# A 13x13 depthwise convolution by Toeplitz matmuls: weights of the last rows widened to 128 columns, patch halves requested together, shifted copies dropped

## The reference, cut to what matters

```python
# layer 0: 1x1 qkv convolution, 2x2 max pool, 3x3 depthwise, channel attention, projection (not touched)
x = x + _L0_conv_ref(_gn(x), ...)
# layer 1: what the changed stage computes, x is (1, 384, 192, 192) fp32
out = _bn(_dwconv(x, w_large, 6), ...) + _bn(_dwconv(x, w_small, 1), ...) + _bn(x, ...)   # w_large (384,1,13,13), w_small (384,1,3,3)
x = x + out(_gn(x))
```

## Time and profile before

| | |
|---|---|
| median of 3 runs | 2976.05 us (2973.62 to 2976.38) |
| the profiled execution's own time | 2976.38 us |
| its span | 2974.7 us |
| PE busy | 2670.8 us (90%) |
| DVE busy | 2522.6 us (85%) |
| ACT busy | 1481.1 us (50%) |
| bytes moved by DMA | 546.95 MB |

### The profile page before, as it was taken

One profiled execution on the slowest core, in us unless ns is written; L12 is line 12 of the kernel. 1 busy time (PEld: TensorE's weight loads), 2 busy tenths in 40 slices (PEclk: granted clock), 3 DMA queues, 4 the chain that ended last, 5 costly groups with the idle time before them and its releaser, 6 DMA issues. The chain is left out here.

```text
span 2974.7 us, 50705 instructions
## 1 busy us (share of the span) xinstructions
PE 2670.8 (90%) x17273; PEld 1812.0 (61%) x17273; DVE 2522.6 (85%) x3512; ACT 1481.1 (50%) x1921; POOL 73.9 (2%) x143
## 2 busy tenths in 40 slices
PE   0049999999999999999995999983999999999998
PEld 0036666666666666666663566652777777777776
DVE  7969999999999999999997898984877777777774
ACT  0033445555554554553232667673655555555553
POOL 0010000000000000000000000000000000000000
PEclk9999999999999999999997999995999999999999
DMA  8964112222322322321004999988999999999985
GB/s 333 416 204 144 49 56 93 85 87 84 103 77 93 103 77 87 100 81 48 17 1 152 333 349 346 343 291 177 251 263 261 261 262 261 261 262 260 262 249 169
DMA packets 349112, 546.95 MB, mean 184 GB/s; under 512 B 143392, under 2 KB 254752, under 8 KB 345888
## 3 DMA queue, kind: packets, MB, share of 16 engines
q1 hardware_dynamic: 317504, 436.49, 47.5%
q10 hardware_dynamic: 31456, 108.48, 11.8%
HBM read 364.47 MB, written 180.44 MB: 183 GB/s over the span
## 5 line engine op out<-in xcount | busy, mean ns | idle before, releaser
L781 PE MATMUL qk_qb<-qk_xhi,whi 128*128 128x384 f16 x2592 | 846.4, 327 | 21.0 <-DVE qk_xlo L677 14.3
L781 PE MATMUL qk_qb<-qk_xlo,whi 128*128 128x384 f16 x2592 | 846.2, 326 | 0.0
L781 PE MATMUL qk_qb<-qk_xhi,wlo 128*128 128x384 f16 x2592 | 846.2, 326 | 0.0
L698 DVE SCALAR_TENSOR_TENSOR qk_dw<-qk_pool,qk_wd,qk_dw 128x768 f32<-128x768 f32 (+2 forms) x864 | 836.9, 1009 | 0.1
L685 DVE TENSOR_REDUCE qk_pool<-qk_qb 128x192 f32<-128x768 f32 x432 | 411.9, 954 | 68.7 <-PE qk_qb L781 51.9
L1491 ACT ACTIVATE cv_res<-cv_cb,cv_cst 128x288 f32<-128x288 f32 x384 | 189.8, 502 | 381.5 <-PE cv_cb L1634 331.3
L1628 PE MATMUL cv_cb<-cv_hi,cv_toep 128*128 128x288 f16 x1536 | 346.6, 286 | 35.5 <-DVE cv_lo_last L1559 32.8
L781 PEld LDWEIGHTS qk_qb<-qk_xhi,whi 128*128 128x128 f16 x2592 | 254.0, 98 | 184.2 <-DVE qk_xlo L677 17.5
L781 PEld LDWEIGHTS qk_qb<-qk_xhi,wlo 128*128 128x128 f16 x2592 | 253.9, 98 | 168.4 <-issue 1.2
L1634 PE MATMUL cv_cb<-cv_hi_next,cv_toep 128*128 128x288 f16 x1536 | 356.3, 293 | 0.0
L781 PEld LDWEIGHTS qk_qb<-qk_xlo,whi 128*128 128x128 f16 x2592 | 254.0, 98 | 162.8 <-issue 1.0
(11 more groups left out here) (163 smaller groups left out, 3466.3 us busy)
## 6 DMA issues: line engine op xcount, KB each, us to landing
cv_toep<-toeplitz_scratch SPq DMA_DIRECT2D x384, 256.0 KB, 4.7
patch_scratch<-pr_turned SPq DMA_DIRECT2D x75, 832.0 KB, 9.6
st_x<-in_x SPq DMA_DIRECT2D x24, 2304.0 KB, 17.1
qk_xf<-in_x SPq DMA_DIRECT2D x72, 768.0 KB, 4.3
pr_xb<-in_x SPq DMA_DIRECT2D x24, 2304.0 KB, 10.1
out<-cv_rows ACTq DMA_DIRECT2D x72, 768.0 KB, 5.7
cv_raw<-patch_scratch SPq DMA_DIRECT2D x25, 1300.0 KB, 9.8
cv_raw<-patch_scratch ACTq DMA_DIRECT2D x23, 1300.0 KB, 9.5
```

Of the source, the lines that this page charges most:

```text
L698: V.scalar_tensor_tensor(acc, pool[:, o, r + y:r + y + n, x:x + PW], wd[:, o, k:k + 1], acc, ALU.mult, ALU.add).then_inc(taps_done, 1)
L781: ins = nc.tensor.matmul(qbank[s % NQB][:, h, 0:2 * W], w[:, b, o * P:(o + 1) * P], x[:, par, j // 2, b, at_row:at_row + 2 * W], start=n = ...
```

## The change

Three edits, all in `stage_depthwise`:

1. `late` gets a second half per channel, filled once with zeros by POOL. The weight view `few` then has 128 columns (64 real, 64 zero), and the three matmuls of row shift 2 write all 128 partitions of the bank. SP waits once for the zeros.
2. `hi_next`, `lo_next` and the copies `next_rows` go. The six matmuls of row shift 1 read `hi` and `lo` at row offset 1 of the pitch-26 rows.
3. SP requests its half of `raw` at c == 9 (behind the load of channel 8's weights) and ACT requests its half at c == 0 (right behind the first eviction, ahead of `last_high` of part 3).

```diff
-        hi_next = sb("hi_next", [P, GRP, TJ, OI], F16)
-        lo_next = sb("lo_next", [P, GRP, TJ, OI], F16)
-        late = sb("late", [P, GRP, ERUN], F16)
+        late = sb("late", [P, GRP, 2, ERUN], F16)
...
-                sp.dma_start(late[:, part_of(q), :],
+                sp.dma_start(late[:, part_of(q), 0, :],
...
-                    if c == GRP // 2 and (inner or g + 2 < NG):
+                    if c == NTOEP + 1 and (inner or g + 2 < NG):
                         address(sp, (g + 2) * (TI * GRP * TJ))
                         sp.wait_ge(edge_done, g * NPC + NPC)
                         start.load_half(sp, g + 2, par, 0)
                     if inner or g < NG:
                         load_taps(g, c)
+                        if at(g, 0) and c == 0:
+                            sp.wait_ge(late_zero, 1)
...
+        @block.gpsimd
+        def _(gp):
+            nc.gpsimd.memset(late[:, :, 1, :], 0.0).then_inc(late_zero, 1)
...
-                    if c == 0:
-                        last_high(g, NPC - 1)
-                    if c == GRP // 2 - 3 and (inner or g + 2 < NG):
+                    if c == 0 and (inner or g + 2 < NG):
                         address(act, (g + 2) * (TI * GRP * TJ))
                         act.wait_ge(edge_done, g * NPC + NPC)
                         start.load_half(act, g + 2, par, 1)
+                    if c == 0:
+                        last_high(g, NPC - 1)
...
-            def next_rows(g, q):
-                V.tensor_copy(hi_next[:, part_of(q)], hi[:, part_of(q), :, 1:1 + OI]).then_inc(hi_next_done, 1)
+            def last_low(g, q):
                 dve.wait_ge(lo_done, g * NPC + q + 1)
-                V.tensor_copy(lo_next[:, part_of(q)], lo[:, part_of(q), :, 1:1 + OI]).then_inc(lo_next_done, 1)
...
-                few = late[:, c, :].rearrange("p (m v) -> p v m", v=2)
+                few = late[:, c].rearrange("p r (m v) -> p v (r m)", v=2)
-                    nc.tensor.matmul(upper, few[:, part], x[:, c, :, 0:EI], start=False, stop=False, skip_group_check=True)
+                    nc.tensor.matmul(whole[:, :, 0:EI], few[:, part], x[:, c, :, 0:EI], start=False, stop=False, skip_group_check=True)
                 for u in range(NU):
-                    for k, (part, x) in enumerate(((0, hi_next), (0, lo_next), (1, hi_next))):
-                        ins = nc.tensor.matmul(whole, taps[:, 1, u * 2 + part], x[:, c, u:u + OJ, :],
+                    for k, (part, x) in enumerate(((0, hi), (0, lo), (1, hi))):
+                        ins = nc.tensor.matmul(whole, taps[:, 1, u * 2 + part], x[:, c, u:u + OJ, 1:1 + OI],
...
-                            for ready in (hi_next_done, lo_next_done, hi_last_done, lo_last_done):
+                            for ready in (hi_last_done, lo_last_done):
```

More of the change, by code:

```diff
@@ L1368, in stage_depthwise @@
         bbank = [ctx.enter_context(nc.psum_tensor(f"cv_bb{i}", [P, 512], F32)) for i in range(NBB)]
-        cst_in = sem("cst_in")
+        cst_in, late_zero = sem("cst_in"), sem("late_zero")
         toep_in = [sem(f"toep_in{i}") for i in range(NTOEP)]
@@ L1373, in stage_depthwise @@
         norm_done, edge_done, hi_done, lo_done = sem("norm_done"), sem("edge_done"), sem("hi_done"), sem("lo_done")
-        hi_next_done, lo_next_done, hi_last_done, lo_last_done = (sem("hi_next_done"), sem("lo_next_done"),
-                                                                  sem("hi_last_done"), sem("lo_last_done"))
+        hi_last_done, lo_last_done = sem("hi_last_done"), sem("lo_last_done")
         conv_done, res_done, back_done, rows_done = (sem("conv_done"), sem("res_done"), sem("back_done"),
@@ L1548, in low @@
                                 ALU.subtract).then_inc(lo_done, 1)
-            def next_rows(g, q):
-                V.tensor_copy(hi_next[:, part_of(q)], hi[:, part_of(q), :, 1:1 + OI]).then_inc(hi_next_done, 1)
+            def last_low(g, q):
                 dve.wait_ge(lo_done, g * NPC + q + 1)
-                V.tensor_copy(lo_next[:, part_of(q)], lo[:, part_of(q), :, 1:1 + OI]).then_inc(lo_next_done, 1)
-            def last_low(g, q):
                 for u in range(NU):
@@ L1575, in split @@
                 low(g, q)
-                next_rows(g, q)
                 last_low(g, q)
@@ L1622, in channel @@
                 taps = toep[:, c % NTOEP, :].rearrange("p (s m v) -> p s v m", s=NS, m=P)
-                few = late[:, c, :].rearrange("p (m v) -> p v m", v=2)
+                few = late[:, c].rearrange("p r (m v) -> p v (r m)", v=2)
                 whole = bank[:, 0:NPIX].rearrange("p (j i) -> p j i", j=OJ)
-                upper = bank[0:HP, 0:NPIX].rearrange("p (j i) -> p j i", j=OJ)[:, :, 0:EI]
                 for u in range(NU):
```

## The result

The changed kernel takes 2940.3 us (median of 4 runs, 2939.52 to 2940.88) against 2974.8; the ratio is 0.9885 (95% interval 0.9868 to 0.9902). That is faster, as forecast, but by 34 us where 88 were forecast, and outside the range of 2875 to 2925. The profiled execution has a span of 2938.3 us, 36.4 less than before.

What follows compares the result with a forecast made beforehand. PE alone was taken to bound the depthwise stage. Span 2974.7 - 94 (widened weights) + 5 (halves together) + 0 (start) = 2885.7 us, a median time of 2887; range 2875 to 2925.

Steps and rivals of the forecast that it cites:

- What bounds the kernel: Depthwise stage from about 2089 us on: PE alone sets the pace; DVE and ACT have room, DMA engines 8% left.
- Widened weights, 94 us: Row shift 2 matmuls: removing both width changes saves 0.25 us per channel over 376 channels, 94 us (bounds 92 and 98).
- No shifted copies, "I take nothing for it": Row shift 1 matmuls reading at an odd fp16 element: no cost taken; dropping DVE's copies worth nothing in the steady state.
- half-rate rival: Row shift 1: PE reads odd-offset rows at half rate, 276 us more, time 3158; chance 0.12.
- Patch halves together, 0.2 us per group: Channel 9's weights land late behind both halves: 0.2 us per group taken, 5 us in all (bounds 0 to 22).
- Start of the stage, 0: First depthwise channels: 3.4 us gained without copies is spent waiting for channel 9's weights; 0 taken, 3.4 either way.
- The range: Whole kernel: 2875 to 2925 us; high end takes in poor DMA meshing and the word per row with its stalls.
- the word per row: Row shift 1: each odd-offset row costs one more word, 0.01 us per matmul, 23 us, time 2910; chance 0.12.
- the late weights: Channel 9's Toeplitz weights behind both patch halves: PE waits at most 1 us per group, 22 us over 22 groups.
- the 5 in the sum: Depthwise stage: 5 us added to the forecast time for PE's waits caused by requesting the patch halves together.
- DMA-bound rival: Depthwise groups: busy DMA time cannot be compressed, a group takes 34.3 us, time 2906, up to 2920; chance 0.12.

Runs made afterwards that it cites:

- b_nocopy: Kernel before with only the shifted copies dropped, row shift 1 read at an odd element: 3000.76 us, ratio 1.0088.
- b_small_patch: Kernel before with widened weights only, and patch loads from group 2 on cut to their first row tile of 25: 2881.03 us, ratio 0.9685.
- b_widen: Kernel before with only the widened 128-column weights for row shift 2; copies kept, halves requested apart: 2891.29 us, ratio 0.9719; 2889.29 us in five more rounds.
- a_stagger: Changed kernel with the third edit undone, so patch halves are requested apart as before: 2912.62 us, ratio 0.9792.
- a_stag_even: Changed kernel with halves requested apart and row shift 1 reading at even row offset 0 instead of 1: 2886.49 us, ratio 0.9706.
- b_together: Kernel before with only the third edit, both patch halves requested after channel 0: 2977.67 us, ratio 1.0007.

## Why the prediction was wrong

- **What bounds the kernel**: right. PE alone; DVE's copies were worth nothing (b_nocopy).
- **Widened weights, 94 us**: right. 0.49 to 0.37 is seen directly. By the mean distances between the starts of matmuls from 2300 to 2800 us a channel is 0.243 us shorter and not 0.25, which makes 91 us. The 93 us of b_small_patch are these 91 and 2.5 us by which its channel 9 starts earlier (2086.7 us instead of 2089.2); b_widen has 83 to 85, by its waits. The drain on a change of tiling mode that the Trainium skill states (TensorEngine Tiling (Array Packing), Key Properties) agrees: with one mode throughout, both gaps went.
- **No shifted copies, "I take nothing for it"**: the first step that failed. The bound given beside it, 0.01 us per matmul and 23 us, was the right one (0.80 instead of 0.74 for six; 26 us in b_nocopy and between a_stagger and a_stag_even, 3 of them not placed). The argument for zero took DVE's reads at the same offset as evidence for PE. They were another engine's. The remark under the half-rate rival, that nothing else in the trace explains why packed shifted copies were kept, was the better evidence and should have decided against zero.
- **Patch halves together, 0.2 us per group**: the second step that failed, and the larger. The method was right: half issued, landing of the weights behind it, need of PE. In it the landing was taken as 18.1 us after channel 0 and is 19.5. Channel 0 ends at 2497.63 + 1.91 = 2499.5 (the chain's matmuls of the group before end at 2497.63). SP's half is issued 1.8 us later and not 1.0, because SP is held until 2500.1 by its issue of the late weights (2498.51, 1.56 us long), which was left out of what is queued ahead; and the weights land 17.7 us after the half's issue, not 17.1. (The medians of 21 groups are much the same: 1.9, 17.7 and together 19.6.) Need is at 1.91 + 7 x 2.34 = 18.3, so 1.2 us late per group (20 waits of 1.3 were measured) where 0.4 came out of the sum and 0.2 was taken. PE's next six matmuls then take 0.92 instead of 0.74, 0.18 more, so that the price per group is 1.4 to 1.5.
- The Trainium skill (SBUF — State Buffer, "Can I just issue two DMAs to hit both halves?") says that two such DMAs serialize and gain 6%. That they serialize agrees with the trace: SP's half lands after 17.3 us instead of 9.8. The 6% can't be read from it, since the rate hangs on the window and on what else moves: 241 GB/s from 2502 to 2510.5 with both halves in flight, 204 from 2503 to 2510, and 187 from 2511.5 to 2517 with SP's alone.
- **Start of the stage, 0**: near, but partly by luck. The prediction took 8 channels as done before 2089.18 us; the trace has 9, and it is channel 9 that starts there. So the need for channel 9's weights was put 2 us too late (2087.6; channel 8 ended at 2085.5), and their landing 1.4 us too late (2091; it was 2089.62), and the errors nearly cancel. PE got there 3.7 us earlier, waited 4.2 us and started channel 9 at 2089.67, 0.5 us later than before. The wait had a second price: in the 5 us from 2089 the mean granted clock is 0.66, a part of it at the 1.2 GHz level, and twice six matmuls take 1.44 us. Together with the start that is 2 us lost.

```profile
2089.67 0.93 PE cv_cb L1624 x6
2090.59 0.62 PE cv_cb L1627 x3
2091.21 1.44 PE cv_cb L1630 x6
2092.65 1.44 PE cv_cb L1624 x6
2094.09 0.38 PE cv_cb L1627 x3
```

- **The sum again, by measured terms**, from the start of channel 9 on, which leaves 375 channels: 91 for the width, less 23 for the offset (375 x 0.06), less 25.5 of waits, less 20 x 0.18 = 3.6 after them, less 0.5 and 1.6 at the start: 37 us, against 36.4 between the spans.
- **The range**: each loss stood there as a rival or a bound of its own, 2910 for the word per row, 22 us at most for the late weights. They come from independent edits and both came true. The high end of 2925 is 15 us above 2910, so with the 5 in the sum it left 20 us for the late weights, where 25.5 + 3.6 in the groups and 2 at the start were measured.
- **The DMA-bound rival** at 2906 to 2920 fell for the reason that it named: the busy share is not incompressible. b_widen ran a group in 33.4 us at a share of 1.01.

## What to carry to other kernels

Price a deadline from the end of the work that releases the request, through every instruction queued ahead of it on the issuing engine, to the moment of need; then move it by a margin larger than its error, since a faster engine moves the need towards it (the halves together cost nothing at the old pace, b_together, and 28 us at the new one, a_stagger against the changed kernel). Where a kernel keeps a copy whose only effect is on how rows lie, suspect that it pays for the reading engine until a row of that engine says otherwise. The best version found is edit 1 alone, 2889 to 2891 us, 3% under the kernel before and 50 us under the change with all three edits.

## What was not expected of the hardware

- A matmul that reads many short runs, each from an odd fp16 element, pays about 0.8 ns per run; one long run from an odd element pays nothing (0.80 against 0.74 us for six).
- After a wait of 1.3 us for weights at full clock the next six matmuls took 0.92 us instead of 0.74, so a short wait costs 0.18 us more than it lasts; after one of 4.0 us they took 1.63, at the lower clock.
- DMA engines at a share of 1.00 in a_stagger carried 284 GB/s, at 1.01 in b_widen 290, and at 0.92 before 261: a share of 0.92 was not 8% but at least 11% in bytes short of what they can carry.
